# Second layer of a two-layer attention kernel: the first score group moved in front of the first values

## The reference

```python
xn = layer_norm(x, norm_w, norm_b)
q = (xn @ q_w + q_b).reshape(Bx, Tx, H, -1)
k = (xn @ k_w + k_b).reshape(Bx, Tx, H, -1)
att = jnp.einsum('bnhl,bmhl->bnmh', q, k)
att = att + (1.0 - mask) * -1000000.0
att = jax.nn.softmax(att, axis=2)
v = ((xn @ v_w + v_b) * src_mask[:, :, None]).reshape(Bx, Tx, H, -1)
y = jnp.einsum('bnmh,bmhl->bnhl', att, v).reshape(Bx, Tx, Dx)
e = jax.nn.silu(emb) @ emb_w + emb_b
scale, shift = jnp.split(e[:, None, :], 2, axis=2)
h = layer_norm(y, sb_norm_w, sb_norm_b) * (1.0 + scale) + shift
h = jax.nn.silu(h) @ out_w + out_b
return x + h
```

## Time and profile before

| | |
|---|---|
| Median of 3 runs | 2234.18 us (2233.34 to 2234.28) |
| Profiled execution | 2234.86 us, of which the span of its instructions is 2233.1 us |
| TensorE matmul busy | 2177.2 us (97%) |
| VectorE busy | 1399.5 us (63%) |
| ScalarE busy | 906.3 us (41%) |
| GpSimd busy | 549.2 us (25%) |
| Granted TensorE clock, mean over the span | 0.984 |

### The profile page before, as it was taken

The page is one execution under the profiler, slowest core; times in us unless marked ns, Lnnn a source line. Parts: engine busy times, 40 slices in busy tenths (PEclk is TensorE's granted clock), DMA queues, the critical chain, the costliest instruction groups (busy, mean ns, idle before and its releaser), DMA issues.

```text
span 2233.1 us, 53651 instructions
## 1 busy us (share of the span) xinstructions
PE 2177.2 (97%) x20991; PEld 1880.3 (84%) x20991; DVE 1399.5 (63%) x3001; ACT 906.3 (41%) x2086; POOL 549.2 (25%) x879
## 2 busy tenths in 40 slices
PE   6899999999999999997999999999999999999997
PEld 3788888888888888885888888888888888888886
DVE  4677777777777777775455564655555564645554
ACT  2233333333333333333344444444454444445444
POOL 0323333332233333322121212212121212222120
PEclk8899999999999999997999999999999999999999
DMA  7211110001111001001010100001010100001000
GB/s 254 86 38 38 38 38 28 33 33 38 38 38 38 33 28 38 33 29 48 2 38 19 38 24 33 28 28 38 19 38 19 38 24 33 28 28 38 19 30 20
DMA packets 51447, 85.17 MB, mean 38 GB/s; under 512 B 5588, under 2 KB 14482, under 8 KB 51416
## 3 DMA queue, kind: packets, MB, share of 16 engines
q1 hardware_dynamic: 51416, 84.73, 10.7%
HBM read 51.03 MB, written 33.69 MB: 38 GB/s over the span
## 4 chain that ended last, share of the span: by engine, by line
PE 51%; DVE 1%; ACT 1%; issue 0%; DMA 0%; POOL 0%; DVEq 0%; SPq 0%; ACTq 0%
PE bank L462 6%; PE bank L453 6%; PE bank L463 6%; PE bank L464 6%; PE bank L455 5%; PE bank L454 5%; PE bank L1428 5%; PE bank L1454 3%; PE bank L1460 2%; PE bank L1471 2%; PE bank L1394 1%; PE bank L1387 1%; PE bank L1444 1%; PE bank L1486 1%; PE bank L1494 0%; ACT prob L1305 0%
## 5 line engine op out<-in xcount | busy, mean ns | idle before, releaser
L462 PE MATMUL bank<-xT_hi,w_hi 128*128 128x256 f32 x1536 | 446.9, 291 | 4.5 <-DVE xT_lo L1151 3.3
L463 PE MATMUL bank<-xT_lo,w_hi 128*128 128x256 f32 x1536 | 442.1, 288 | 0.0
L464 PE MATMUL bank<-xT_hi,w_lo 128*128 128x256 f32 x1536 | 438.9, 286 | 0.0
L453 PE MATMUL bank<-w_hi,xT_hi 128*128 128x512 f32 x768 | 318.5, 415 | 0.0
L455 PE MATMUL bank<-w_lo,xT_hi 128*128 128x512 f32 x768 | 309.7, 403 | 0.0
L462 PEld LDWEIGHTS bank<-xT_hi,w_hi 128*128 128x128 f32 x1536 | 290.7, 189 | 20.3 <-issue 8.0
L454 PE MATMUL bank<-w_hi,xT_lo 128*128 128x512 f32 x768 | 306.6, 399 | 0.0
L463 PEld LDWEIGHTS bank<-xT_lo,w_hi 128*128 128x128 f32 x1536 | 291.2, 190 | 1.2
L464 PEld LDWEIGHTS bank<-xT_hi,w_lo 128*128 128x128 f32 x1536 | 291.4, 190 | 0.0
L810 ACT ACTIVATE k_exp<-bank,k_neg 128x128 f32<-128x128 f32 x256 | 72.8, 369 | 370.7 <-DVE k_neg L695 368.4
L453 PE MATMUL bank<-w_hi,h_hi 128*128 128x512 f32 x512 | 217.4, 425 | 3.8 <-DVE h_lo L1213 3.7
(11 more groups left out here) (181 smaller groups left out, 4067.0 us busy)
## 6 DMA issues: line engine op xcount, KB each, us to landing
xr<-in_x SPq DMA_DIRECT2D x32, 512.0 KB, 3.4
x_between_layers<-x SPq DMA_DIRECT2D x64, 256.0 KB, 2.0
xr<-x_between_layers SPq DMA_DIRECT2D x32, 512.0 KB, 3.6
out<-y_out SPq DMA_DIRECT2D x64, 256.0 KB, 2.0
raw<-in_L_cond_W_emb SPq DMA_DIRECT2D x4, 1024.0 KB, 12.3
raw<-in_L_cond_emb_w SPq DMA_DIRECT2D x4, 1024.0 KB, 8.2
mask_rows<-mask_parts SPq DMA_DIRECT2D x128, 2.0 KB
raw<-in_L_cond_Wq SPq DMA_DIRECT2D x1, 1024.0 KB, 5.4
```

Of the source, the lines that this page charges most:

```text
L453: yield nc.tensor.matmul(bank[:, :], a_hi[:, c, b, :], w_hi[:, m, c, :], start=(c == 0), stop=False)
L462: yield nc.tensor.matmul(dst, w_hi[:, m, c, fs], a_hi[:, c], start=(first and c == 0), stop=False)
L463: yield nc.tensor.matmul(dst, w_hi[:, m, c, fs], a_lo[:, c], start=False, stop=False)
L464: yield nc.tensor.matmul(dst, w_lo[:, m, c, fs], a_hi[:, c], start=False, stop=(c == C - 1))
```

## The change

On TensorE `scores(i, 0)` moves up, from behind the values of b = 0 and the transposes of z to directly behind `mixed(i - 1, 1)`. VectorE's list is rewritten: the four maxima of b = 0 come earlier, each in front of another step, and `end_silu(i - 1, 0)` with `low_part(i - 1, 0)` comes later. Nothing is added or removed. The new file is two lines longer, so its lines behind 1246 are numbered one to two higher.

```diff
@@ VectorE, body @@
             if not first:
                 end_outputs(i - 1, 0)
                 end_norm(i - 1, 0)
+            maxima(i, 0, (0,))
+            if not first:
                 end_outputs(i - 1, 1)
+            maxima(i, 0, (1,))
             values(i, 0, first)
-            maxima(i, 0, (0,))
+            if not first:
+                end_norm(i - 1, 1)
+            maxima(i, 0, (2,))
             if not first:
                 end_silu(i - 1, 0)
-                end_norm(i - 1, 1)
-            maxima(i, 0, (1,))
-            if not first:
                 low_part(i - 1, 0)
             values(i, 1, first)
-            maxima(i, 0, (2, 3))
+            maxima(i, 0, (3,))
@@ TensorE, body @@
             if not first:
                 mixed(i - 1, 1, C + 4)
+            scores(i, 0, first)
             values0 = value_rows(i, 0, first)
             run(islice(values0, 4))
             woven(values0, () if first else turned(i - 1, 1))
             if not first:
                 z_transposed(i - 1, 0)
-            scores(i, 0, first)
             run(value_rows(i, 1, first))
```

More of the change, by code:

```diff
@@ L1245, in body @@
                 end_norm(i - 1, 0)
-                end_outputs(i - 1, 1)
-            values(i, 0, first)
             maxima(i, 0, (0,))
             if not first:
+                end_outputs(i - 1, 1)
+            maxima(i, 0, (1,))
+            values(i, 0, first)
+            if not first:
+                end_norm(i - 1, 1)
+            maxima(i, 0, (2,))
+            if not first:
                 end_silu(i - 1, 0)
-                end_norm(i - 1, 1)
-            maxima(i, 0, (1,))
-            if not first:
                 low_part(i - 1, 0)
             values(i, 1, first)
-            maxima(i, 0, (2, 3))
+            maxima(i, 0, (3,))
             if not first:
```

## The result

| | before | after |
|---|---|---|
| Median of 5 runs | 2234.28 us | 2288.1 us (2286.53 to 2288.61) |
| Ratio | | 1.0234, 95% interval 1.022 to 1.0248 |
| Span of the profiled execution | 2233.1 us | 2284.7 us |
| One pair of layer 2 | 35.98 us | 37.59 us |

What follows compares the result with a forecast made beforehand. TensorE was taken as the bound, with nearly no idle time. 30 x 1.69 + 1.84 + 0.5 = 53.0 us on the profiled 2234.86 gave 2287.9, and 0.7 less for the median 2287.2 us; range 2274 to 2297.

Steps and rivals of the forecast that it cites:

- its 6 us: TensorE over 31 pairs: one change of tile form fewer saves at most 0.20 us a pair.
- the wait for y: TensorE before the values of b = 1: the whole 0.20 us gain is lost there, net 0.
- The unseen step: TensorE from the probability-value group straight into scores, shown by no row: taken as 0.20 us, bounds nothing to 0.40.
- h_lo waits 1.69 us a pair: TensorE before out_rows(i - 1, 0): stands still from 1655.14 to 1656.83 because VectorE's and ScalarE's steps deliver h_lo later.
- First pair +0.5: First pair: scores wait 1.0 us for ScalarE's copy of the queries, a later maxima wait shrinks; net +0.5 us.
- Last pair +1.84: Last pair: without x_transposed before the output projection, TensorE arrives earlier and waits about 0.15 us more, 1.84.
- The sum: Whole kernel: 30 x 1.69 + 1.84 + 0.5 = 53.0 us added to the profiled execution.
- Rival 1: Only the data chain counts, VectorE's queue not delaying the silu: 0.75 us a pair, 2258 us; chance 8%.
- Rival 2: Faster: last transposed output to h_lo fits in 4.8 us, TensorE keeps the saved change of form, 2228.5 us; chance 4%.
- Rival 3: The loop's clock falls too: each new TensorE gap brings 8 us at half speed, about 2411 us; chance 5%.

Runs made afterwards that it cites:

- e5_covered: Changed kernel with z's transposes (b = 0) directly behind the scores, transposed outputs woven in earlier, three maxima before end_outputs(i - 1, 1), silu right behind it: 2228.88 us.
- e1: Changed kernel with VectorE's part of the diff taken back, so TensorE's new order runs with VectorE's old list: 2268.44 us, 1.0147 of the kernel before.
- e4: Changed kernel with the transposes of z for b = 0 moved up to directly behind the scores: 2298.45 us, 1.0284 of the kernel before.
- e3_max_first: Changed kernel with all four maxima of b = 0 on VectorE ahead of end_outputs(i - 1, 1): 2261.91 us, 1.0117 of the kernel before.

## Why the prediction was right

- *TensorE is the bound, and its 6 us are lost to the wait for y.* Right. The values of b = 1 load 5.33 us behind the scores (1595.63 to 1600.96), predicted 5.32 (1646.15 to 1651.47), and the wait for y is there. The 0.20 us that the move was to save by itself was not measured alone; e5_covered, which changes more, keeps 0.25 us a pair. The prediction's own rows give less for the step into the scores (0.17 listed as idle, or 0.20 less the usual 0.11 between starts), so 0.20 was a generous price; no term of the sum hangs on it, since the wait for y takes it all.
- *The unseen step costs 0.20.* Right, 0.20 idle. The Trainium skill (TensorEngine Tiling (Array Packing), Key Properties) says that a change of tiling mode drains TensorE. The trace agrees as far as it goes: an idle time of 0.20 us stands at this step; what fills it no row shows.
- *h_lo waits 1.69 us a pair.* The mechanism is right, confirmed by taking it apart in e1 to e4; the size was a little too high: the wait listed is 1.57 us, 0.12 less, and TensorE arrives at it 0.05 later than the prediction had it (9.04 behind the scores, not 8.99). The chain from reciprocal to TensorE's load was put at 6.39 us and took 6.32: behind the aggregate a maximum follows after 0.09, not the 0.14 read from the values in that place, the values follow that maximum after 0.57, not 0.60, and the rest is a hundredth here and there. Pair: 37.59 against 37.67.
- *First pair +0.5.* The waits are right: from the last load of the query projection to the first of the next pair's keys it takes 13.53 us (1072.57 to 1086.10), before 13.09 (1074.02 to 1087.11), 0.44 more. But 1.5 us more went to the half clock, which the prediction put at nothing: the stretch behind takes 5.98 us where it took 4.49. The rows are of before, then of after:

```profile
1087.11 0.19 PEld L462 LDWEIGHTS bank<-xT_hi,w_hi 128*128 128x128 f32 x1 [1.98 <-DVE top L1171]
...
1091.60 0.19 PEld L462 LDWEIGHTS bank<-xT_hi,w_hi 128*128 128x128 f32 x1
```

```profile
1086.10 0.19 PEld L462 LDWEIGHTS bank<-xT_hi,w_hi 128*128 128x128 f32 x1 [1.97 <-DVE top L1171]
...
1092.08 0.19 PEld L462 LDWEIGHTS bank<-xT_hi,w_hi 128*128 128x128 f32 x1
```

- *Last pair +1.84.* The wait for h_lo there is 2.0 us, the 1.84 and the 0.16 that was there before.
- *The sum.* The spans differ by 51.6 us where 53.0 was predicted. The pairs bring 30 x 0.08 = 2.4 less and the first pair 1.4 more. Two terms lie outside the mechanism: the new profile reaches the end of the first query projection 1.45 us sooner, before anything that the change touches, and its tail is 0.9 longer. The last wait for h_lo ends at 2222.49 us before and at 2273.07 after; some 4 us behind it the clock is back at 1.00 before (2226.4 to 2227.1) and still 0.50 after (2277 to 2278.6). Together this gives 51.5. The rows of VectorE that wait for that projection, of before and then of after:

```profile
2227.13 0.69 DVE L1222 TENSOR_TENSOR y_out<-bank,xr 128x512 f32<-128x512 f32 x1 [2.70 <-PE bank L455]
```

```profile
2278.65 0.69 DVE L1222 TENSOR_TENSOR y_out<-bank,xr 128x512 f32<-128x512 f32 x1 [3.65 <-PE bank L455]
```

  The runs of the changed kernel alone lie 2 us apart (2286.53 to 2288.61). So it is partly luck that the median came within 0.9 us of 2287.2; the pair, 37.59 against 37.67, is what bears the prediction out.
- *Rivals.* Rival 1 needed the silu at its data's time; it is 0.9 us behind it. In e3_max_first, where it is nearly so, the kernel comes to 2262 (rival 1 said 2258). Rival 2 needed a chain, from the last transposed output to TensorE's load, under 4.8 us; it is 6.6 (1599.62 to 1606.24). Rival 3: the clock of the loop stayed 1.00 through gaps of 1.57 us in each pair. The page that spoke for it (TensorE: Matmul & The Clock Gate of the Trainium skill, A second HAM failure mode: psum-queue depth-cycling) is not borne out by such gaps here.

What stays open: why the clock falls once in the first pair. It goes with the early scores there. Of the two longest waits of TensorE ahead of the dip, 0.97 and 1.8 us, the second stands in the kernel before too; the first does not (0.54 is the next longest there). Whether that wait brings the dip about was not tested apart from the order of the scores.

## What to carry to other kernels

When a block moves up on a saturated engine, everything it passes comes later by its length; follow each passed result through the in-order lists of the other engines to the next wait, and compare with the slack there, since here some 6 us of expected saving met 54.6 us of such waits. Counting the instructions on VectorE between "data ready" and "data used", at start-to-start distances from the trace, gave the loss to 0.08 us a pair. Here the move paid only when the producers moved too: work with slack (maxima) into idle time, and the heads of the long chains (transposes of z, transposed outputs) earlier.

## What the runs showed of the hardware that was not expected

- The granted clock was 0.50 from 1087.7 to 1090.9 us in the changed kernel, behind waits of 0.97 us and 1.8 us of TensorE in the first pair, while 30 gaps of 1.57 us, one in each 37.6, left it at 1.00.
- A wait can be listed as "issue": 29.0 us in front of line 1394 in e1_pe_only were waits for VectorE's norm.
